# Loading a tile's adjacency as stripes of 512 columns in place of 2048 neighbouring columns

## The reference

```python
q, k, v = x @ Wq + bq, x @ Wk + bk, x @ Wv + bv        # n, 4 heads, 32 channels
attn = einsum('nhc,mhc->hnm', q, k) / sqrt(32)          # only where adj[n, m] != 0
out = einsum('hnm,mhc->hnc', softmax(attn), v)
x_r = x @ Ws + bs
beta = sigmoid(concat([out, x_r, out - x_r]) @ Wb)
return layernorm(x + beta * x_r + (1 - beta) * out)
```

## Time and profile before

| | us |
|---|---|
| median of 3 runs | 1975.72 (1969.99 to 1978.83) |
| the profiled execution | 1964.78 |
| its span, first to last instruction | 1962.9 |
| busy: DVE | 1310.3 (67%) |
| busy: POOL | 1174.4 (60%) |
| busy: PE | 1164.9 (59%) |
| busy: ACT | 839.9 (43%) |

### The profile page before, as it was taken

How to read it: one execution, slowest core, us unless ns; L and a number is a source line. 1 busy time by engine, 2 the same in 40 slices (tenths; PEclk the granted TensorE clock), 3 DMA queues, 4 the chain that set the end, 5 groups by cost and what they waited for, 6 DMA issues and landing times.

```text
span 1962.9 us, 20126 instructions
## 1 busy us (share of the span) xinstructions
PE 1164.9 (59%) x4696; PEld 680.4 (35%) x4696; DVE 1310.3 (67%) x3389; ACT 839.9 (43%) x1595; POOL 1174.4 (60%) x1711
## 2 busy tenths in 40 slices
PE   7322746657574756466655657756766668444553
PEld 5101433334342334233323334423423334233342
DVE  5876878666756776557656468757555677886564
ACT  2331443334643463344634348545635476431112
POOL 4454565566566656656566656565665665676664
PEclk9565677677776776667777578876667767666565
DMA  9947856666755776564866668776767778433331
GB/s 334 354 164 199 318 198 233 214 233 223 293 197 183 258 271 234 216 218 161 342 230 215 247 243 294 265 258 247 252 217 278 249 255 280 140 89 96 94 89 57
DMA packets 130037, 438.70 MB, mean 223 GB/s; under 512 B 26567, under 2 KB 61198, under 8 KB 97150
## 3 DMA queue, kind: packets, MB, share of 16 engines
q1 hardware_dynamic: 76510, 297.15, 41.1%
q0 software_dynamic: 52832, 136.07, 22.5%
q10 hardware_dynamic: 576, 4.19, 0.5%
HBM read 417.93 MB, written 19.44 MB: 223 GB/s over the span
## 4 chain that ended last, share of the span: by engine, by line
POOL 34%; issue 24%; DVE 13%; DMA 13%; PE 7%; DVEq 4%; another core or an unknown queue 3%; ACT 2%; SPq 1%; ACTq 0%; POOLq 0%
POOL s_kv L799 31%; DMA s_kv<-kv_rows,s_rec_in 11%; DVE s_raw L1248 2%; DVE s_kv L1246 2%; PE s_acc L1001 1%; DVEq L1296 1%; DVE s_wtop L1295 1%; POOL node_records L766 1%; POOL out_rows L775 1%; ACT s_mask L1023 1%; DVEq L1443 1%; DVE s_kv L1272 1%; DVE s_d_max L1454 1%; PE s_ps_key L889 1%
## 5 line engine op out<-in xcount | busy, mean ns | idle before, releaser
L799 POOL DMA_INDIRECT s_kv<-kv_rows,s_rec_in x1023 | 1024.3, 1001 | 700.6 <-DMA s_kv<-kv_rows,s_rec_in 340.6
L829 PE MATMUL s_ps_w<-s_mask,s_bit_w 128*128 128x512 bf16 x1008 | 374.6, 521 | 332.4 <-ACT s_mask L1023 233.8
L1023 ACT ACTIVATE s_mask<-s_adj_in 128x2048 bf16<-128x2048 f32 x252 | 478.2, 1900 | 114.5 <-DMA s_adj_in<-in_adj 66.7
L1001 PE MATMUL s_acc<-s_kv,ident 128*128 128x128 f32 x2032 | 321.3, 330 | 109.9 <-DVE s_kv L1272 62.8
L1001 PEld LDWEIGHTS s_acc<-s_kv,ident 128*128 128x128 f32 x2032 | 312.2, 244 | 137.4 <-DVE s_kv L1272 77.3
L829 PEld LDWEIGHTS s_ps_w<-s_mask,s_bit_w 128*128 128x128 bf16 x1008 | 111.3, 120 | 559.1 <-ACT s_mask L1023 294.9
L1246 DVE TENSOR_TENSOR s_kv<-s_kv,s_ps_q 128x1536 f32<-128x1536 f32 (+15 forms) x76 | 147.1, 1935 | 235.2 <-DMA s_kv<-kv_rows,s_rec_in 224.3
L1272 DVE TENSOR_TENSOR s_kv<-s_kv,s_ps_q 128x1536 f32<-128x1536 f32 (+15 forms) x76 | 146.7, 1931 | 17.9 <-ACT s_ps_q L1062 10.1
L1062 ACT ACTIVATE s_ps_q<-s_sc 128x56 f32<-128x56 f32 (+17 forms) x76 | 16.7, 220 | 318.4 <-DVE s_sc L1262 218.5
L1248 DVE TENSOR_REDUCE s_raw<-s_kv 128x48 f32<-128x1536 f32 (+15 forms) x76 | 147.1, 1935 | 5.6
L1050 ACT COPY s_xs<-s_ps_x 128x128 f32<-128x128 f32 x63 | 16.6, 264 | 288.7 <-remote 160.4
(11 more groups left out here) (281 smaller groups left out, 1563.2 us busy)
## 6 DMA issues: line engine op xcount, KB each, us to landing
s_adj_in<-in_adj SPq DMA_DIRECT2D x248, 1024.0 KB
s_kv<-kv_rows,s_rec_in POOLq DMA_INDIRECT x1023
kv_rows<-s_kv SPq DMA_DIRECT2D x16, 512.0 KB, 7.6
s_rec_in<-node_records SPq DMA_DIRECT2D x55, 106.0 KB
s_kv<-in_x_cols SPq DMA_DIRECT2D x4, 1024.0 KB, 8.4
s_adj_in<-in_adj ACTq DMA_DIRECT2D x4, 1024.0 KB
s_d_in<-in_x_cols SPq DMA_DIRECT2D x8, 512.0 KB
s_d_v<-kv_rows SPq DMA_DIRECT2D x8, 512.0 KB
```

The lines of the kernel that those rows point to most:

```text
L799: nc.gpsimd.indirect_dma_start(out=kv[0:n, START[k] + s], out_offset=None, in_=kv_dram[:, :], in_offset=bass.IndirectOffsetOnAxis(ap=rec_i ...
L829: last = nc.tensor.matmul(w[:], bit_w[:, slab], mask[:, k % 2, s * WORD:(s + 1) * WORD], start=False, stop=(slab == SLABS - 1))
L1001: last = nc.tensor.matmul(acc[:, c * D:(c + 1) * D], ident[:], kv[:, START[k] + s, D:2 * D], start=(s == 0), stop=(s == plain(k) - 1))
L1023: nc.scalar.activation(mask[:, q % 2], adj_in[:, q % ADJ_RING], ACT.Sign, accum_out=edges[:, t, h:h + 1]).then_inc(masked, 1)
```

## The change

A part of a tile's adjacency is made of the four 512-column stripes `h`, `h + 4`, `h + 8`, `h + 12`, which lie 2048 columns apart, in place of 2048 neighbouring columns. They are put side by side in the same 8 KB of the `adj_in` slot, so that the mask's instruction, the sizes and the number of loads stay. `pack_part` multiplies the s-th slice of part `h` by the weight of slab `4 s + h`, so that the packed words are the same. No wait is added on SP.

```diff
+        def adj_part(t, h):
+            rows = adj[t * P:(t + 1) * P, :].rearrange("p (s h c) -> p s h c", s=SLABS_A_PART, h=PARTS)
+            return rows[:, :, h]
+
+        def adj_place(r):
+            return adj_in[:, r].rearrange("p (s c) -> p s c", s=SLABS_A_PART)
+
...
-                sp.dma_start(adj_in[:, q % ADJ_RING], adj[t * P:(t + 1) * P, h * PART:(h + 1) * PART]
+                sp.dma_start(adj_place(q % ADJ_RING), adj_part(t, h)
                              ).then_inc(adj_loaded[q % ADJ_RING], 16)
...
                 for s in range(SLABS_A_PART):
-                    slab = h * SLABS_A_PART + s
+                    slab = s * PARTS + h
...
             for q in range(PARTS):
-                act.dma_start(adj_in[:, q], adj[P:2 * P, q * PART:(q + 1) * PART]).then_inc(adj_loaded[q], 16)
+                act.dma_start(adj_place(q), adj_part(1, q)).then_inc(adj_loaded[q], 16)
```

## The result

| | before | after |
|---|---|---|
| median, us | 1974.05 (8 runs, 1969.99 to 1979.43) | 1990.49 (8 runs, 1986.57 to 1995.22) |
| ratio after / before | | 1.008, 95% interval 1.0063 to 1.0097 |
| profiled execution and its span | 1964.78; 1962.9 | 1986.57; 1984.7 |

The change makes the kernel 0.8% slower. The forecast was 1906 us, its range ended at 1982.

What follows compares the result with a forecast made beforehand. POOL's pauses for gathers delayed by adjacency were taken as the bound: 58 us gained in the first stretch plus 14 in the second is 72, say 70, off the 1975.72 us median, giving 1906 us; range 1855 to 1982.

Steps and rivals of the forecast that it cites:

- What bounds the kernel: Chain of waits: POOL's alone from 66 to 1050 us, through DVE, ACT and PE to 1720; adjacency costs POOL 192 us.
- I count half of POOL's gain: Second stretch, 1050 to 1720 us: the chain is not POOL's, so 14 us of POOL's 29 us gain count.
- I take one half of the excess, since the pile-up should go as well as the bare turns: POOL's pauses beside adjacency: half of what adjacency adds goes, 64 us in the first stretch and 32 in the second.
- the bare turns: Lower bound in POOL's pauses: three shorter adjacency packets between a gather's own save 0.69 us a pause, 32 and 21 us.
- if by bytes it stays: Adjacency handed to an engine ahead of a gather: held by count it shrinks with the piece, held by bytes it stays.
- Only makes adjacency be in flight about a tenth longer: Adjacency queue: 2 KB pieces at 87 ns add 61 us an engine, hidden; longer flight takes 6 and 3 us from POOL.
- dearer pieces: Slower rival, chance 0.13: skipping in HBM makes 2 KB pieces cost more; gain eaten from about 130 ns, middle 2010 us.
- Absorbed: Rival, chance 0.15: pauses stay under 64 KB turns, or shrink while DVE, ACT and PE keep pace; 1970 to 1989 us.
- one for one: DMA queues, both full: one adjacency packet goes between any two gather packets; expected near again with 2 KB pieces.
- SP's issue ... at most 0.1 us x 248: SP's adjacency loads: issue takes 434 ns against 328, under SP's 685 us of waits for masks; counted at nothing.
- ACT's start at nothing: ACT's adjacency waits before 200 us, 48.5 us: a tenth more is 5 us, counted as nothing since the chain is POOL's.
- By count throughout: Rival, chance 0.12: all that adjacency adds to POOL's pauses shrinks by 73%; gain 117 us, 1858 us.

Runs made afterwards that it cites:

- r11: The kernel before with POOL pausing after each 11 gathers in place of 12 (RUN = 11); ratio 1.013, 1995.32 us.
- g8: The kernel before, whole 8 KB rows, with SP waiting for each adjacency load to land before issuing the next; ratio 0.9716, 1918.29 us.
- p8: The kernel before, whole 8 KB rows, with each SP adjacency load held by a table until a POOL pause has ended; ratio 0.9389, 1853.77 us.
- n2: The kernel before with all 252 loads in 2 KB pieces, neighbours in HBM, kept apart by interleaved SBUF slots; ratio 0.9935, 1961.81 us.
- e1: The changed kernel with stripes for SP's 248 loads only, ACT's four loads whole 8 KB rows as before; ratio 1.0073, 1987.35 us.
- e2: The changed kernel with stripes for ACT's four loads only, SP's 248 loads whole as before; ratio 1.0048 against before, 1980.79 us.
- e3: SP's loads in two stripes of 1024 columns (4 KB pieces), ACT's whole, against the kernel before; ratio 0.9875, 1949.48 us.
- i2: The changed kernel's stripes, 8 KB apart in HBM, put into interleaved SBUF slots; ratio 1.0074 against before, 1982.89 us.
- d2: The changed kernel with 2 KB stripes beginning 4 KB apart in HBM in place of 8 KB; ratio 1.0074 against before, 1978.69 us.

## Why the prediction was wrong

- **What bounds the kernel: right, and more so than it said.** POOL's pauses set the end (r11, g8, p8). The half for the second stretch ("I count half of POOL's gain") was too little by p8, whose span fell by 110 us, more than its waits for landings (91); r11 is nearer to the forecast's caution. It didn't matter to the miss.
- **The step that failed: "I take one half of the excess, since the pile-up should go as well as the bare turns".** It was worth 64 + 32 us. The turns did shrink (first packet to landing 1.6 to 1.3 us), but a gather's first packet comes 0.8 us later, 3.4 for 2.6, and a lone gather lands after 4.3 us for 4.1. What stands ahead is 56 to 75 KB an engine in pieces of the three sizes, and no less of it with short ones. Loaded pauses stayed at 5.7 us, where the forecast had 3.4. The prediction named this case ("if by bytes it stays") and gave it a weight of half. It was all of it, with the turns taken back too. n2 shows this step nearly alone: its pieces cost about what the forecast took (52 us more in the queue for 61), and its ratio is 0.9935, some 0.003 of it the slow start, where the forecast's is 0.965.
- **"Only makes adjacency be in flight about a tenth longer": mis-sized.** At least 8 engines are at such pieces for 909 us for 792, 15% longer, and 59 pauses are loaded for 54. Loaded pauses thus take 337 us for 308, the others 95 for 107: that is the 17 us. The price was part of it: 99 ns a stripe, just above the bound of 98, for the 87 taken, and 346 for 8 KB in the mean of the whole trace, where one window gave 318. Four stripes cost 50 ns more than a row of 8 KB and not 30, and by 2016 rows an engine that is the queue's 102 us in place of 61. A skip in HBM is dearer than a neighbour (93). The "dearer pieces" rival had this direction right and the size wrong: it turned at 130 ns and had the DMA engines full.
- **Absorbed: its time was nearest (1970 to 1989; measured 1990), its reason was half right.** The pauses stayed and the longer flight made more of them loaded, as it said. But a turn of 64 KB isn't what the trace shows. Strung together by end and start (the trace doesn't name the engine, so this is a reconstruction), an engine's packets after the change run: gather, one stripe, gather, one stripe, count, then mostly 8 to 11 stripes until the next gather comes. So the one for one that the prediction wanted to see again holds between a gather's own packets, and not in the totals, here from 81 to 86 us after the change, against the earlier trace rows:

```profile
q1 hardware_dynamic: 682, 1.35, 75.3%
q0 software_dynamic: 191, 0.52, 29.2%
```

By the Trainium skill (DMA: Bandwidth & Descriptors, Queues, rings and completion order) a turn is typically 9 to 17 descriptors and 64 at most. By that, 32 stripes would be more than one typical turn, and not one as the prediction had it; and a gather's three packets would go in one. The reconstructed order, with one stripe between them, disagrees. Ahead of a gather's first packet 35 stripes pass, more than is typical and within the page's ceiling.

- **"SP's issue ... at most 0.1 us x 248" and ACT's start at nothing: wrong.** A load takes SP 540 ns for 328, 0.21 more; e1 has it too, and no run shows what it costs beside SP's waits for masks (758 us after the change). ACT's four were not priced at all, and they stand ahead of `bit_w`: 6 us of start, over a quarter of the span's 22 (e2: 1.0048). The row that warned was the earlier trace rows, 3.4 us for a load behind one with many pieces, which the prediction used for SP only.
- **By count throughout** is refuted by e3 and n2 too: 18 pieces of 4 KB and 32 to 35 of 2 KB go ahead of a gather, not 7. Its one support, that e3's ratio came near the rival's 0.98, isn't explained by what stands ahead.

## What to carry to other kernels

When one queue's transfer waits behind another's, ask first how much is queued ahead of it: here that was 56 to 75 KB an engine, and cutting it in shorter pieces made it no less and made it last longer. Moving the bulk transfer away from the wait (loads issued behind the pause, or fewer of them in flight) gained 2.5 to 6% with whole rows, and with short pieces 2% at best and lost 3.5% at worst. Cutting it gained 1.3% at best, at 4 KB, and lost at 2 KB stripes. Price an issue on every engine that issues it, and look at what stands behind it in that engine's program.

## What the hardware showed that I had not expected

- Between the issue of a lone gather and its first packet, a full hardware queue moves 56 to 75 KB an engine in the median and 87 at most: 7 pieces of 8 KB, 18 of 4 KB, 32 to 35 of 2 KB. With at most 64 KB an engine in flight (g8) it is 49 KB, and the loaded pause is 4.4 us for 5.7.
- 2 KB pieces with a gap of 2 or 6 KB between them in HBM take 98 to 100 ns in the mean, neighbouring ones 93; the medians are 84. Pieces of 4 KB take 177 ns in the mean, 8 KB 346, so by bytes 4 KB is hardly dearer than 8.
- Four loads of 512 short pieces in a row stall the engine that issues them: 7.69 us for 2.00, 5.5 of them in one (ACT, at the start).
- The same gated kernel gained 6.1% on one chip and 2.5% on another. No ungated kernel was repeated on a second chip; three with ungated stripes (e1, i2, d2) gave 1.0073, 1.0074 and 1.0074 on two.
